# Gated cross attention with a mixture of experts on one core: the second norm of three batches inside the attention, the shared experts by halves of the tokens, second biases as spare rows

## The reference

```python
x = x + tanh(g_xattn[0]) * xattn(layernorm(x), ctx, pos, pos, Wq, Wkv, Wout, bout)
x = x + tanh(g_ffn[0]) * ffn(layernorm(x), ...)

def expert(xf, w1, b1, w2, b2):              # 256 -> 176 -> 256
    return maximum(xf @ w1 + b1, 0.0) @ w2 + b2

def ffn(x):
    shared = sum(expert(x, sw1[e], sb1[e], sw2[e], sb2[e]) for e in range(2)) / 2
    probs = softmax(x @ router_w + router_b)             # 32 routed experts
    p, i = top_k(probs, 6)
    gates = zeros; gates[i] = p / sum(p)
    return shared + sum(gates[:, e] * expert(x, rw1[e], rb1[e], rw2[e], rb2[e]) for e in range(32))
```

## Time and profile before

| | |
|---|---|
| median of three executions | 455.83 us (455.70 to 456.46) |
| the profiled execution | 456.51 us |
| its span | 454.7 us |
| mean granted clock of PE | 0.996 of 2.4 GHz |
| busy: PE, weight loads, DVE, ACT, POOL | 435.1, 338.2, 279.5, 196.0, 141.4 us |

### The profile page before, as it was taken

How to read it: one execution, slowest core, us unless ns; L and a number is a source line. 1 busy time by engine, 2 the same in 40 slices (tenths; PEclk the granted TensorE clock), 3 DMA queues, 4 the chain that set the end, 5 groups by cost and what they waited for, 6 DMA issues and landing times.

```text
span 454.7 us, 7925 instructions
## 1 busy us (share of the span) xinstructions
PE 435.1 (96%) x2489; PEld 338.2 (74%) x2489; DVE 279.5 (61%) x585; ACT 196.0 (43%) x375; POOL 141.4 (31%) x231
## 2 busy tenths in 40 slices
PE   8778999999999899999989999999999999999996
PEld 5556777677677557676878888888888888888884
DVE  7989887787787746615445445545555544455555
ACT  6986878578578563622222222222222222222221
POOL 8359300000000011532433444443333334444430
PEclk9999999999999999998999999999999999999999
DMA  7211111111011008949994443333323333333102
GB/s 217 77 29 42 36 37 33 27 36 35 23 39 33 16 1 224 286 107 277 334 215 114 112 98 96 92 92 92 92 92 96 97 112 93 105 97 93 46 0 92
DMA packets 34102, 43.59 MB, mean 96 GB/s; under 512 B 5681, under 2 KB 28257, under 8 KB 34081
## 3 DMA queue, kind: packets, MB, share of 16 engines
q1 hardware_dynamic: 33041, 43.31, 34.5%
q10 hardware_dynamic: 1040, 0.01, 0.1%
HBM read 37.93 MB, written 1.18 MB: 86 GB/s over the span
## 4 chain that ended last, share of the span: by engine, by line
PE 86%; DVE 4%; DMA 3%; ACT 3%; SPq 2%; issue 1%; DVEq 0%; ACTq 0%
PE psum L1210 27%; PE psum L1227 26%; PE psum L1037 7%; PE psum L1073 7%; PE psum L1061 6%; PE psum L1023 3%; DMA G<-gates_by_expert 2%; PE psum L1126 2%; PE psum L1048 1%; PE psum L984 1%; PE psum L974 1%; PE psum L1085 1%; DVE nmax L795 1%; PE psum L944 1%; ACT probs L542 1%; SPq L336 1%
## 5 line engine op out<-in xcount | busy, mean ns | idle before, releaser
L640 ACT ACTIVATE hh<-hu 128x512 fp32r<-128x512 f32 x88 | 55.6, 633 | 189.8 <-DVE hu L913 189.8
L913 DVE SCALAR_TENSOR_TENSOR hu<-psum,b1cols,G 128x512 f32<-128x512 f32 x88 | 65.8, 750 | 112.8 <-PE psum L1210 100.1
L795 DVE TENSOR_REDUCE nmax<-psum 128x2 f32<-128x512 f32 x128 | 82.8, 686 | 14.8 <-PE psum L1037 14.7
L542 ACT ACTIVATE probs<-psum 128x512 f32<-128x512 f32 x128 | 66.3, 604 | 26.9 <-PE psum L1061 26.9
L1227 PE MATMUL psum<-hh,w2h 128*128 128x512 f32 (+1 forms) x188 | 73.5, 391 | 1.4 <-DVE hl L919 1.4
L1227 PE MATMUL psum<-hh,w2l 128*128 128x512 f32 (+1 forms) x188 | 73.3, 390 | 0.0
L1227 PE MATMUL psum<-hl,w2h 128*128 128x512 f32 (+1 forms) x188 | 73.2, 390 | 0.0
L919 DVE SCALAR_TENSOR_TENSOR hl<-hu,hh 128x512 fp32r<-128x512 f32 x88 | 60.8, 693 | 9.6 <-ACT hh L640 9.6
L452 POOL CAST w2h<-w 128x256 fp32r x44 | 17.9, 406 | 134.4 <-PE psum L1227 134.4
L1210 PE MATMUL psum<-xTh,w1l 128*128 128x512 f32 (+1 forms) x188 | 58.7, 394 | 0.0
L1210 PE MATMUL psum<-xTh,w1h 128*128 128x512 f32 (+1 forms) x188 | 58.7, 394 | 0.0
(11 more groups left out here) (152 smaller groups left out, 546.9 us busy)
## 6 DMA issues: line engine op xcount, KB each, us to landing
G<-gates_by_expert SPq DMA_DIRECT2D x40, 256.0 KB, 4.0
w<-in_L_ffn_rw_dram SPq DMA_DIRECT2D x4, 1408.0 KB, 11.6
w<-in_L_ffn_rw_dram SPq DMA_DIRECT2D x2, 2816.0 KB, 19.2
G<-gates_by_expert SPq DMA_DIRECT2D x8, 448.0 KB, 3.6
Kd<-QK SPq DMA_DIRECT2D x104, 32.0 KB, 1.8
G<-gates_by_expert SPq DMA_DIRECT2D x8, 384.0 KB, 3.7
G<-gates_by_expert SPq DMA_DIRECT2D x8, 320.0 KB, 3.6
G<-gates_by_expert SPq DMA_DIRECT2D x8, 192.0 KB, 3.8
```

Source lines behind the costliest of these rows:

```text
L542: act.activation(probs[g % 2][:, kt, 2 * hp:2 * hp + 2, :], ST_BANK[(4 * g + n) % 3][:, :].rearrange("p (h q) -> p h q", h=2), ACT.Exp, sc ...
L640: act.activation(hh[(SHT + j) % 2][:, cols], hu[2 * j + half][:, :], ACT.Relu).then_inc(rhh_ok, 1)
L795: dve.tensor_reduce(nmax[i % 2][:, qt, 2 * hp:2 * hp + 2], S_BANK[n % 2][:, :].rearrange("p (h k) -> p h k", h=2), AX.X, ALU.max, negate=T ...
L913: dve.scalar_tensor_tensor(out=hu[2 * (j % 2) + half][:, :], in0=H_BANK[2 * (j % 2) + half], scalar=b1cols[:, bass.ds(it * len(G) + j, 1)] ...
```

## The change

- **Second norm.** `residual(b)` ends with `variances` of its batch. For batches 0 to 2, POOL makes the whole of the norm (`second_rows`), PE transposes the rows in steps 25, 26 and 30 of the attention (`ROWS_STEPS`), ACT copies them in the same step, and POOL rounds and splits them (`split_rows`). Batch 3 stays behind the loop, on the DVE.
- **Shared experts.** Instead of tile by tile, they are made in six pieces of one half of the tokens (`SHARED`, pairs of tile and half), put between the steps of the last batch. All calls of `keep_warm` from step 33 on are gone.
- **Second biases.** `rb2` fills rows 96 to 127 of the last shared weight tile, and the gates fill the same rows of its hidden tile (`hu[2]`, `hu[3]`). So the result block of that tile adds them. `sb2` is averaged by two small matmuls against `mean`, put into `b1cols`, and added in the last copies to `yT`. The four matmuls of L1265 are gone.
- **Memory.** The buffers of the later part are moved. `load_weights(0)` now waits for the last values (`pv_mm`) instead of the last normalisation.

The core of the diff:

```diff
-        b1cols = sb("b1cols", [P, TILES])
+        b1cols = sb("b1cols", [P, TILES + KD])
         b1half = sb("b1half", [P, SHT])
-        b2_sb = sb("b2_sb", [NE + NS, D])
+        sb2_sb = sb("sb2_sb", [NS, D])
+        mean = sb("mean", [NS, 1])
...
+        ROWS_STEPS = [GROUPS - 7, GROUPS - 6, GROUPS - 2]
+
+
+        SHARED = [(0, 0), (1, 0), (2, 0), (1, 1), (0, 1), (2, 1)]
+        SHARED_HU = [0, 1, 2, 0, 1, 3]
...
-            sp.dma_start(b2_sb[0:NE, :], rb2).then_inc(b2_ld, 16)
-            sp.dma_start(b2_sb[NE:NE + NS, :], sb2).then_inc(b2_ld, 16)
+            sp.dma_start(sb2_sb[:, :], sb2).then_inc(b2_ld, 16)
...
+            sp.dma_start(w2s[SREST:P, SFULL, :], rb2).then_inc(ws_ld, 16)
...
-            sp.wait_ge(norm_ok, PAIRS)
+            sp.wait_ge(pv_mm, GROUPS)
...
-                sp.dma_start(gd[:, cols], gTf[0:NE, cols]).then_inc(gd_st, 16)
+                sp.dma_start(gd[:, cols], hu[2 + half][SREST:P, :]).then_inc(gd_st, 16)
...
-            def shared_low_part(u):
-                t, half = u // 2, u % 2
...
+            def shared_low_part(n):
+                t, half = SHARED[n]
                 cols = slice(half * HALF, (half + 1) * HALF)
-                pool.wait_ge(hh_ok, u + 1)
-                pool.tensor_tensor(hl[t % 2][0:rows, cols], hr[half][0:rows, :], hh[t % 2][0:rows, cols],
+                pool.wait_ge(hh_ok, n)
+                pool.tensor_tensor(hl[t % 2][:, cols], hu[SHARED_HU[n]][:, :], hh[t % 2][:, cols],
                                    ALU.subtract).then_inc(hl_ok, 1)
...
-            inverse_root(4, slice(0, NT - TB))
-            pool.wait_ge(norm_ok, PAIRS)
-            pool.memset(gates[:, :, NE:NE + NS], 1.0 / NS).then_inc(half_ok, 1)
-            inverse_root(5, slice(NT - TB, NT))
-            pool.wait_ge(xn2_ok, NT)
-            for b in (0, 2, 3):
+            def second_rows(b):
+
+                rows = slice(TB * b, TB * b + TB)
+                inverse_root(4 + b, rows)
+                pool.wait_ge(root_ok, 4 + b)
+                then(pool.tensor_tensor(newton[:, rows], rough[:, rows], rough[:, rows], ALU.mult))
+                then(pool.tensor_tensor(newton[:, rows], newton[:, rows], veps[:, rows], ALU.mult))
+                then(pool.tensor_scalar(newton[:, rows], newton[:, rows], -0.5, 1.5, ALU.mult, ALU.add))
+                then(pool.tensor_tensor(rstd[:, rows], rough[:, rows], newton[:, rows], ALU.mult))
+                if b >= 2:
+                    pool.wait_ge(x2T_mm, b - 1)
+                for t in range(TB):
+                    n = TB * b + t
+                    pool.tensor_scalar(xn2[b % 2][:, t, :], x_sb[:, n, :], mv[:, n, 0:1], rstd[:, n:n + 1],
+                                       ALU.subtract, ALU.mult).then_inc(xn2_ok, 1)
+
+            def split_rows(b):
                 cols = slice(TB * b * P, TB * (b + 1) * P)
+                pool.wait_ge(x2T_ok, b + 1)
+                pool.tensor_copy(xTh[:, :, cols], xT32[:, :, cols]).then_inc(xh_ok[b // (B // 2)], 1)
                 pool.wait_ge(xh_ok[b // (B // 2)], b % (B // 2) + 1)
                 pool.tensor_tensor(xTl[:, :, cols], xT32[:, :, cols], xTh[:, :, cols], ALU.subtract).then_inc(xl_ok[b // (B // 2)], 1)
 
-            for u in range(2):
-                shared_low_part(u)
+            second_rows(0)
+            second_rows(1)
+            split_rows(0)
+            split_rows(1)
+            second_rows(2)
+            split_rows(2)
+            pool.wait_ge(norm_ok, PAIRS)
+            pool.memset(gates[:, :, 0:SREST], 0.0).then_inc(blank_ok, 1)
+            inverse_root(3 + B, slice(NT - TB, NT))
+            shared_low_part(3)
+            shared_low_part(4)
...
+                if i in ROWS_STEPS:
+                    second_rows(ROWS_STEPS.index(i))
...
+                if b:
+                    act.wait_ge(pj_mm, b)
+                else:
+                    act.wait_ge(lo_ok, 2 * B)
+                act.activation(attnT[:, :, :, :], C_AT[b].rearrange("p (t k q) -> p t k q", t=TB, k=KD), ACT.Copy).then_inc(aT_ok, 1)
 
...
+            for i in range(GROUPS + 2):
+                if i == GROUPS + 1:
+                    act.wait_ge(b1_ok, 2)
+                step(i)
+            shared_relu(0)
+            shared_high_part(0)
+            transposed_attention(B - 1)
+            shared_relu(1)
+            shared_high_part(1)
...
-            shared_relu(0)
-            shared_high_part(0)
-            shared_relu(1)
+            shared_relu(2)
+            shared_relu(3)
+            shared_high_part(3)
+            shared_relu(4)
+            shared_high_part(4)
             act.wait_ge(sub_ok, 1)
             act.activation(ex[:, :, :], ex[:, :, :], ACT.Exp).then_inc(pexp_ok, 1)
-            shared_high_part(1)
-            for u in range(2, 4):
-                shared_relu(u)
-                shared_high_part(u)
+            shared_relu(5)
             act.wait_ge(gT_mm, 1)
-            act.activation(gTf[:, 0:HALF], GT_BANK[0][0:NE + NS, :], ACT.Copy).then_inc(gTf_ok[0], 1)
-            for u in range(4, 6):
-                shared_relu(u)
-                shared_high_part(u)
+            act.activation(hu[2][SREST:P, :], GT_BANK[0][SREST:P, :], ACT.Copy).then_inc(gTf_ok[0], 1)
+            shared_high_part(2)
+            shared_high_part(5)
...
+                variances(TB * b, TB)
...
-            inverse_deviations(0, NT - TB)
-            for b in range(B - 1):
-                normalise_rows(b, xn2[:, b], xn2_ok)
...
+            shared_low_part(0)
+            shared_low_part(1)
             residual(B - 1)
-            variances(NT - TB, TB)
+            roots[0] += B - 1
             inverse_deviations(NT - TB, TB)
-            normalise_rows(B - 1, xn2[:, B - 1], xn2_ok)
-            cols = slice(TB * P, 2 * TB * P)
-            dve.wait_ge(xh_ok[0], 2)
-            dve.tensor_tensor(xTl[:, :, cols], xT32[:, :, cols], xTh[:, :, cols], ALU.subtract).then_inc(xl_ok[0], 1)
+            normalise_rows(B - 1, xn2[(B - 1) % 2], xn2_ok)
+            cols = slice((NT - TB) * P, NT * P)
+            dve.wait_ge(xh_ok[1], 2)
+            dve.tensor_tensor(xTl[:, :, cols], xT32[:, :, cols], xTh[:, :, cols], ALU.subtract).then_inc(xl_ok[1], 1)
+            dve.wait_ge(rt_mm, 1)
             dve.memset(lg[:, :, NE:], UNUSED)
-            dve.wait_ge(rt_mm, 1)
...
+            dve.tensor_tensor(gates[:, :, SREST:P], sel[:, :, :], per_expert(red[:, 1]), ALU.mult).then_inc(gates_ok, 1)
+
+            dve.wait_ge(gT_mm, 2)
...
+            pe.wait_ge(b2_ld, 16)
+            pe.wait_ge(half_ok, 1)
+            for k in range(KD):
+                pe.matmul(A_B1[:, TILES + k:TILES + k + 1], sb2_sb[:, k * P:(k + 1) * P], mean[:, :], start=True, stop=True)
...
+            def shared_hidden(n):
+                t, half = SHARED[n]
+                if n >= 2:
+                    pe.wait_ge(relu_ok, n - 1)
+                else:
+                    pe.wait_ge(x2T_ok, B - 1)
+                pe.wait_ge(ws_ok, t * 2 + 1)
+                pe.wait_ge(xh_ok[half], B // 2)
+                pe.wait_ge(xl_ok[half], B // 2)
+                hidden_parts(SHARED_BANK[n % 2], t, P if t < SFULL else SREST, half).then_inc(h_mm, 1)
+
...
+                for half in range(2):
+                    if isinstance(r, int) and r == 0:
+                        if half:
+                            pe.wait_ge(gTf_ok[0], 1)
+                        else:
+                            pe.wait_ge(relu_ok, 2 * SHT)
+                    elif isinstance(r, int) and r == 1:
+                        if half:
+                            pe.wait_ge(gTf_ok[1], 1)
...
+                if i == GROUPS + 1:
+                    shared_hidden(0)
...
+                if i in ROWS_STEPS:
+                    second_rows_transposed(ROWS_STEPS.index(i))
...
-                if i > GROUPS:
-                    keep_warm(3, S_BANK[0])
-
-
-            keep_warm(3, S_BANK[0])
+
+            router_scores(0)
+            outputs(PAIRS - 1)
+            shared_hidden(1)
             attention_transposed(B - 1)
-            keep_warm(4, S_BANK[0])
+            shared_result(0, first=True).then_inc(y_mm, 1)
             output_projection(B - 1)
-
...
-            for b in range(B - 1):
-                second_rows_transposed(b)
-            for b in range(B - 1):
-                router_scores(b)
-            keep_warm(5, O_BANK)
+            router_scores(1)
+            shared_result(1).then_inc(y_mm, 1)
+            router_scores(2)
+            shared_hidden(2)
             second_rows_transposed(B - 1)
-            hidden(0, 0, P, halves=(0,))
             router_scores(B - 1)
+            shared_hidden(3)
             pe.wait_ge(lgT_ok, 1)
             for t in range(TB):
                 ins = pe.transpose(C_RT[:, t * P:(t + 1) * P], lgT[:, t * P:(t + 1) * P], ident[:, :])
             ins.then_inc(rt_mm, 1)
-            hidden(0, 0, P, halves=(1,))
-            pe.wait_ge(lg_ok, TB)
```

(24 more changed lines are left out.)

260 lines of the change are left out of this document (119 added, 141 removed).

## The result

The changed kernel takes **461.94 us** (median of six executions, 460.83 to 464.66) where the kernel before took 456.07 in the same sessions: a ratio of 1.0133, 95% interval 1.0109 to 1.0158. The forecast was slower, at 458.8 with a range of 454.2 to 461.0. So the sign was right and the size too small: +5.9 us instead of +3.0. The executions of the changed kernel spread by 3.8 us; its profiled one is the slowest of the six (464.66, span 462.6, mean clock 0.982), so its landmarks add up to more than the median shows.

The account below looks back on a forecast made before the run. The prediction took the landing of the fifth `G`, queued behind the second expert weights and following the gates, to bound the end. +1.1 to the fifth `G`, +1.8 clock and +0.1 end gave +3.0: 458.8 us, range 454.2 to 461.0.

Parts of the forecast that it names:

- The end hangs on the fifth `G`, and `G` on the gates: Routed experts: the fifth `G`, issued behind the second weights, sets the end and moves with both gate halves.
- Head, +0.44: Start: two f32 matmuls of `sb2` against `mean` ahead of the transpose of `b1rows` cost +0.44 us, bounds 0 and 0.56.
- Variances, +1.44: Attention: two aggregates and `veps` end the residual of three batches, uncovered, 0.48 us each; bounds 0 and 1.44.
- Transposes, +1.2: Attention steps 25, 26 and 30: four more transposes each, 0.41 us per four on TensorE.
- POOL in the attention, 0: Attention: POOL scales and splits three batches at no cost to TensorE; meeting the DVE taken as 0.
- Tail, -2.0: From the last shifted scores to the gates: keep-warm and moved transposes go, waits and blocks come; at best -2.5 us.
- Rival 2: Tail: without keep-warm the clock falls there too, up to 1.8 us more, 1.5 taken, 460.3; chance 0.13.
- Gates to the fifth `G`: From both gate halves being out to the fifth `G`: the queue's work stays the same; both +1.1 us later.
- Biases of the second layer, 0: Ahead of the fifth `G`: eight `b_sb` records (3.63 us) and the slow stretch behind them go, worth 0.
- Waiting and clock, +1.8: Fifth tile: TensorE idles some 6.7 us instead of 1.4 and the clock falls, +1.8 us; bounds 0 and 1.8.
- from there to the end it is TensorE alone, 2.72 us for 12 matmuls: Routed experts behind the fifth `G`: TensorE alone, at 2.72 us for 12 matmuls; no term for a changed rate.

Follow-up runs that it names:

- Experiment 1: Second expert weights issued in three transfers, behind the fifth to seventh `G`, instead of one block ahead of the fifth: changed kernel 454.91 us, kernel before 455.98.
- experiment 4: The kernel before without the four matmuls of `b_sb` against `gTf`, so the second layer's biases are missing from the result: 457.66 us (1.0028).
- changed kernel's second profile: The changed kernel itself run and profiled once more, with nothing changed: 462.24 us (1.0112).
- experiment 6: The changed kernel with aggregates and `veps` of three batches placed behind the next step's row maxima instead of ahead of them: 462.43 us (1.0127).
- experiment 3: The changed kernel with six f32 matmuls of zeros on TensorE within the wait ahead of the fifth tile's result: 462.51 us (1.0127).
- experiment 7: SBUF placement runs: changed kernel with `hu`, `hh`, `hl` above `w1`, `w2` 466.82 us; with operands aligned by 64 bytes 462.03; kernel before, 64 bytes out of line, 458.69.
- shifted kernel before: The kernel before with 64 unused bytes per partition ahead of `attn`, so weights' parts and everything behind lie 64 bytes higher: 457.68 us, one execution.
- first combined version: The changed kernel with second weights in three transfers, head matmuls moved later, first two batches' aggregates behind row maxima, and operands aligned by 64 bytes: 450.38 us (0.9859).
- experiment 5: The changed kernel with the `mean` matmuls and the transpose of `b1rows` behind `transposes(1)` instead of ahead of it: 462.17 us (1.0099).

## Why the prediction was right in sign and wrong in size

- *The end hangs on the fifth `G`, and `G` on the gates*: right. Experiment 1 shows it by removing it, experiment 4 by removing work ahead of it and gaining nothing. The idle time forecast, 6.7, was measured as 6.73, though the landmark moved by 3.24 and not by 1.1: what was too small ahead of the gates moved TensorE and `G` alike. The changed kernel's second profile has 7.58.
- *Head, +0.44*: the matmuls were sized about right (the four records take 0.53, or 0.13 each; the 0.11 is not in the earlier trace rows), the term was not. It is 1.69: the keys' transfer was issued 0.33 later, took 2.60 instead of 1.85, and at 0.50 of the clock behind it 0.6 more went. The bound of 0.56 counted only TensorE's own work on a path that goes on through ACT, SP and a DMA.
- *Variances, +1.44*: 0.31 and 0.38 in the first two steps by experiment 6, and in step 28 a wait longer by 0.36 (1.68 against 1.32 of the earlier trace rows). That is 1.1, near the term. Not in it: behind the longer wait the clock fell in this execution. In the changed kernel's second profile it didn't behind 1.67, and the step from values to values is 3.55 us there (159.26 to 162.81) and 4.84 here: 1.3 us that come in one execution and not in the other.
- *Transposes, +1.2*: right. Steps 25, 26 and 30 are longer by 0.40, 0.43 and 0.44.
- *POOL in the attention, 0*: right, TensorE never waits for it, and its four tiny operations took 0.19 or 0.20 each, as estimated. The terms above leave nothing of the attention's 3.50 for the DVE being held up by POOL. It was close: moved back by a fraction of a step, in experiment 6, the same work made TensorE wait 1.46.
- *Tail, -2.0*: -1.34 (5.19 to 3.85). Every piece was in its place, in the right order and each a little later: the last batch's projection at 180.75 - 5.19 = 175.56 where 175.3 was forecast, its rows transposed at 182.4 (181.9), the result that waits for POOL at 189.7 (189.2), the gates transposed at 193.9 (193.3). Rival 2, a fall of the clock here, did not occur.
- *Gates to the fifth `G`*: taken as unchanged, but 0.6 shorter.
- *Biases of the second layer, 0*: right in substance, and a little worse than that by experiment 4.
- *Waiting and clock, +1.8*: the mechanism was right, by the one trace of experiment 3, the size was 2.47 (5.71 less 3.24). The whole result ran at 1.2 GHz, where the model, was a stretch in which the clock rose on the way. In the second profile the result took 4.68, which is 1.7 over the 3.01 of the earlier trace rows, so the 1.8 was not far off for every execution. The Trainium skill's page "TensorE: Matmul & The Clock Gate" (section "HAM oscillation — how this bites in real kernels") says that TensorE falls back when idle and starts slow; the trace agrees, with a granted clock of 0.50 behind the 6.73 us.
- *The missing term, +2.1 to 2.2*: "from there to the end it is TensorE alone, 2.72 us for 12 matmuls" was read as a constant of the work. It holds for the placement of the tiles, and the change moved them (experiment 7). This is the step that failed most: the rate of the loop was put at no change without a reason, and it is 2.1 us of the 3.1 by which the forecast was too low. With it the forecast would have been 461.0, and the rest, some 0.9, is spread over the head, the falls of the clock and the tail. The head, 1.25 short, is the second.

In the profiled execution the terms add up to 7.8. In the second profile of the changed kernel the same landmarks are later by 2.0 at the first values, 4.0 at step 28's, 4.6 at the end of the fifth tile's result and 6.6 at the last matmul's end, with one fall of the clock less. That the median's 5.9 is made of the same terms is argued from these two; no execution near it was profiled.

## What to carry to other kernels

When the end waits for a transfer, ask what is queued ahead of it before making anything else faster: here 7 us lay in one block of weights that nobody needed for another hundred, and removing work without moving the block made the kernel before 1.2 us slower. A duration copied from the old trace for an untouched loop is a forecast too, if the change moves its operands in SBUF; keep the distance between the stationary and the moving tile as it was, or compare the matmuls in a window of 100 us first. And where TensorE waits some 2 us, count the clock's fall as a chance and not as a yes or no.

## What the runs showed of the hardware that was not expected

- **Three rates of the same matmul at full clock**: 226.7, 228.9 and 233.3 ns for 512 columns, which at 2.4 GHz is 544, 549 and 560 cycles. The middle one is a pattern that repeats every three matmuls, 226, 229 and 232 ns from start to start. All eight profiles with a distance between stationary and moving tile that is a multiple of 256 bytes settled at 226.7 (442 or 443 matmuls in 100 us), all nine that are 64 off at 228.9 (438 or 439) or, in one, 233.3 (430). Why it is so, and whether other distances do it, was not tried. The Trainium skill's page "SBUF — State Buffer" (section "Who interferes with whom") gives TensorE two independent read ports and says that it never waits on anyone. By that the placement should change nothing; here it changes 226.7 to 228.9, and the measurement decides.
- **A wait near 2 us brings the clock down in some executions and not in others.** Behind 1.79 at the first tile it held in the changed kernel and behind 1.89 it fell in experiment 1. Behind 1.67 or 1.68 in step 28 it fell in four profiles of eleven: it fell in the first of the changed kernel and held in its second. It fell behind 2.24 at the fifth tile of the shifted kernel before, and held behind 2.91 in the first combined version. Behind 1.3 to 1.5 it never fell, behind 4.57 and more always. The length of the wait alone doesn't decide: it fell once in the head behind 0.74 (experiment 5), and in the kernel before behind no wait at all (208.10).
- **A 32 KB transfer between tiles took 2.6 to 3.15 us instead of 1.85** in the eight of seventeen profiles in which instruction code was fetched at that time. That the fetch is the cause is argued (experiment 5).
